# Unneeded products in four stage ends, and another order of copies, picks and routing in the latent attention

## The reference, cut to what matters

```python
x = _layernorm(x + L0_attn(x))                 # test-time training
x = _layernorm(x + L0_xattn(x, ctx, ctx))      # cross-attention, 32 query heads, 8 kv heads
x = _layernorm(x + L0_ffn(x))                  # silu(x@gate)*(x@up)@down, 1024 inner
x = _layernorm(x + L1_attn(x))                 # attention along the batch axis, 16 positions, causal
x = _layernorm(x + L1_xattn(x, ctx))           # latent cross-attention, 16 heads
x = _layernorm(x + L1_ffn(x))                  # 64 experts, 6 a token, 48 slots an expert, and a shared one
# L1_xattn: scores = (x Wq w_kc_q W_qr) . (rope(ctx) W_kr); softmax; times rope(ctx); w_kc_kv; Wo
# routing of L1_ffn: sigmoid(x@gate_w); best 4 of 8 groups; best 6 experts;
#   each expert keeps the first 48 of its tokens in token order
```

## Time and profile before

| | |
|---|---|
| time before, median of 3 runs | 1368.23 us (1364.22 to 1368.31) |
| the profiled execution | 1355.45 us, span 1353.6 us |
| mean granted TensorE clock | 0.963 |
| PE busy | 1198.9 us (89%) |
| DVE busy | 960.0 us (71%) |
| ACT busy | 550.5 us (41%) |

### The profile page before, as it was taken

How to read it: one execution, slowest core, us unless ns; L and a number is a source line. 1 busy time by engine, 2 the same in 40 slices (tenths; PEclk the granted TensorE clock), 3 DMA queues, 4 the chain that set the end, 5 groups by cost and what they waited for, 6 DMA issues and landing times. The chain is left out here.

```text
span 1353.6 us, 24642 instructions
## 1 busy us (share of the span) xinstructions
PE 1198.9 (89%) x9167; PEld 778.8 (58%) x9167; DVE 960.0 (71%) x2192; ACT 550.5 (41%) x1473; POOL 252.3 (19%) x327
## 2 busy tenths in 40 slices
PE   8799999999978989798998989886999999679964
PEld 3577788677743333245564457775777777334431
DVE  1699988699976777569984999863447688763325
ACT  3112112444426666564542210014777777232212
POOL 4000000122210111305431000110000000137761
PEclk9899999999989999999998989997999999899998
DMA  6211223200011332070001000006600000459557
GB/s 186 52 51 52 56 74 102 42 2 2 2 47 47 96 96 74 22 144 1 0 1 63 1 1 1 2 1 210 178 17 17 24 21 17 119 155 279 109 97 280
DMA packets 82851, 92.89 MB, mean 69 GB/s; under 512 B 25232, under 2 KB 66214, under 8 KB 82470
## 3 DMA queue, kind: packets, MB, share of 16 engines
q1 hardware_dynamic: 73820, 77.16, 19.4%
q0 software_dynamic: 6784, 10.43, 4.3%
q10 hardware_dynamic: 2128, 3.71, 0.8%
HBM read 68.91 MB, written 22.36 MB: 67 GB/s over the span
## 5 line engine op out<-in xcount | busy, mean ns | idle before, releaser
L400 DVE TENSOR_REDUCE gqa_x_slots<-gqa_scores 128x8 f32<-128x1024 f32 x64 | 78.4, 1226 | 35.3 <-PE gqa_scores L287 35.3
L1498 DVE TENSOR_REDUCE mla_neg_max<-mla_scores 128x8 f32<-128x1024 f32 x32 | 39.2, 1225 | 88.6 <-PE mla_scores L1369 62.8
L1447 ACT ACTIVATE mla_probs<-mla_scores,mla_neg_max 128x128 f32<-128x128 f32 x256 | 90.3, 387 | 6.1 <-DVE mla_neg_max L1498 6.1
L308 PE MATMUL gqa_scoresT<-gqa_x_slotsT,gqa_keys 32*128 32x512 f32 x256 | 72.9, 642 | 17.1 <-issue 15.1
L356 ACT ACTIVATE gqa_expT<-gqa_scoresT 128x1024 f32<-128x1024 f32 x64 | 65.6, 1024 | 38.7 <-PE gqa_scoresT L308 38.7
L2170 PE MATMUL ttt_z_ps<-ttt_prod,ident 128*128 128x256 f32 x288 | 70.9, 403 | 8.7 <-DVE ttt_prod L2246 8.7
L287 PE MATMUL gqa_scores<-gqa_keys_bd,xT 32*128 32x512 f32 x256 | 72.7, 665 | 4.2 <-DVE gqa_x_slots L400 2.3
L2170 PEld LDWEIGHTS ttt_z_ps<-ttt_prod,ident 128*128 128x128 f32 x288 | 55.3, 200 | 22.0 <-DVE ttt_prod L2246 14.7
L1359 PE MATMUL mla_q_ps<-xT,mla_to_keys 128*128 128x128 f32 x512 | 65.3, 283 | 1.5 <-PEq L63 1.5
L1359 PEld LDWEIGHTS mla_q_ps<-xT,mla_to_keys 128*128 128x128 f32 x512 | 62.3, 199 | 2.2 <-issue 2.1
L2177 PE MATMUL ttt_w_ps<-ttt_prod,ttt_neg_ident 128*128 128x144 f32 x448 | 58.9, 291 | 4.9 <-DVE ttt_prod L2279 4.9
(11 more groups left out here) (447 smaller groups left out, 2808.0 us busy)
## 6 DMA issues: line engine op xcount, KB each, us to landing
moe_w_gu<-in_moe_w_gu SPq DMA_DIRECT2D x24, 384.0 KB, 6.1
gqa_keys_bd<-in_gqa_keys_bd SPq DMA_DIRECT2D x16, 512.0 KB, 3.5
moe_w_dn<-in_moe_w_down SPq DMA_DIRECT2D x24, 192.0 KB, 7.0
moe_sums<-moe_zeros SPq DMA_DIRECT2D x2, 2176.0 KB, 11.4
xT<-in_x_feat SPq DMA_DIRECT2D x4, 512.0 KB, 7.4
ttt_k_by_head<-ttt_k_feat SPq DMA_DIRECT2D x8, 256.0 KB, 4.5
ttt_k_seq<-ttt_k_by_head SPq DMA_DIRECT2D x4, 512.0 KB, 3.8
x_tok<-in_mla_woT SPq DMA_DIRECT2D x8, 256.0 KB, 3.3
```

The lines of the kernel that those rows point to most:

```text
L308: ins = nc.tensor.matmul(scoresT[:, j % 2, :], keys[b % NBUF][group, c, :], x_slotsT[group, k % 2, :], start=True, stop=True)
L400: nc.vector.tensor_reduce(x_slots[:, b % 2, :, c * NJ + 2 * half:c * NJ + 2 * half + 2, HD].rearrange("p g j -> p j g"), scores[:, of].rea ...
L1447: ins = nc.scalar.activation(probs[:, k % NB, e, i, :], scores[:, k % 2, e, i, :], ACT.Exp, bias=neg_max[:, k % 2, e, i:i + 1], accum_out= ...
```

## The change

It does six things.

- Cross-attention: at step NU+3, between the last `turn_back` and the norm transposes of sequence 15, three f32 products.
- Feed-forward: eleven bf16 products ahead of the norm transposes of sequence 15.
- Batch axis: the transposes of 13 stand ahead of `out(15)` instead of behind it, with one f32 product between them; two f32 products stand between the transposes of 14 and 15.
- Latent attention, ACT: in steps 0 and 1 `copy_q(k+1)` stands ahead of `exponential(k)`.
- Latent attention, routing: the early picks are made in two parts, 256 keys in steps 20 and 21, and the other 256 with the first 48 results in steps 28 and 29, instead of 512 keys in steps 28 and 29; the first half's keys are turned at step 19 instead of 23; the parts of group 2 are spread otherwise over steps 30 to 34 (part 1 a step earlier, parts 2, 4 and 6 where they leave one later).
- Latent attention: at step 35, two f32 products.

```diff
@@ cross_attention_gqa, PE
                 if 0 <= k - 2 < NU:
                     weigh(k - 2)
+                if k == NU + 3:
+                    keep_busy(nc, scoresT[:, 0, :], keep["ident"][:], keys_bd[1][:, 0].rearrange("p g t -> p (g t)"), 3)
@@ gated_ffn_int8, PE
                 if sequence_at(n - 3) is not None:
+                    if sequence_at(n - 3) == B - 1:
+                        keep_busy(nc, gate_ps[:, 0], w_up[:, 0, 0, 0:P], x_parts[:, 0, 0, 0, :], 11)
                     norm.tensor(pe, sequence_at(n - 3))
@@ batch_axis_attention, PE
+            unused = w_qkv[:].rearrange("p c n -> p (c n)")[:, 0:512]
+            norm.tensor(pe, L - 3)
+            keep_busy(nc, wide_ps[:, 0, :], keep["ident"][:], unused, 1)
             out(L - 1)
-            for n in range(L - 3, L):
-                norm.tensor(pe, n)
+            norm.tensor(pe, L - 2)
+            keep_busy(nc, wide_ps[:, 0, :], keep["ident"][:], unused, 2)
+            norm.tensor(pe, L - 1)
@@ latent_cross_attention
-        ROUTE_LAG = 14
-        PARTS_AT = ((0,), (1, 2), (3, 4), (5, 6), (7,))
-        KEYS_AT, TOP_AT = (23, 27), (28, 29)
+        PARTS_AT = {14: (0, 0), 15: (0, 1, 2), 16: (0, 3, 4), 17: (0, 5, 6), 18: (0, 7),
+                    22: (1, 0), 23: (1, 1, 2), 24: (1, 3, 4), 25: (1, 5, 6), 26: (1, 7),
+                    30: (2, 0, 1), 31: (2, 2), 32: (2, 3), 33: (2, 4, 5), 34: (2, 6, 7)}
+        KEYS_AT = (19, 27)
+        TOP_AT = {20: (0, 0), 21: (0, 1), 28: (1, 0), 29: (1, 1)}
+        KEYS_LO, KEYS_HI = (0, moe.GK), (moe.GK, 2 * moe.GK + moe.CAP)
...
+                if k == LAST - 3:
+                    keep_busy(nc, scores[:, 0, 0].rearrange("t i n -> t (i n)"), keep["ident"][:], to_out[:, 0:2, :].rearrange("p c d -> p (c d)"), 2)
@@ latent_cross_attention, ACT
+                if k < 2:
+                    copy_q(k + 1)
                 if in_range(k):
                     exponential(k)
-                if in_range(k + 1):
+                if k >= 2 and in_range(k + 1):
                     copy_q(k + 1)
@@ latent_cross_attention, DVE
                 if k in TOP_AT:
-                    dve.wait_ge(moe.keys_copied, len(KEYS_AT))
-                    n = TOP_AT.index(k)
-                    for r in range(n * ROUNDS // 2, (n + 1) * ROUNDS // 2):
-                        moe.top_keys(order, moe.keys[:, moe.EARLY:], moe.EARLY, r)
+                    g, half = TOP_AT[k]
+                    dve.wait_ge(moe.keys_copied, g + 1)
+                    for r in range(half * ROUNDS // 2, (half + 1) * ROUNDS // 2):
+                        moe.top_keys(order, moe.keys[:, KEYS_HI[g]:KEYS_HI[g] + moe.CAP], KEYS_LO[g], KEYS_HI[g], r)
```

More of the change, by code:

```diff
@@ L1141, in __init__ @@
         self.zeros = sb("zeros", [P, self.W])
-        self.EARLY, self.PICKS = self.N // 4, self.N // 4 + self.CAP
-        self.keys, self.keys_left = sb("keys_by_expert", [P, self.PICKS]), sb("keys_left", [P, 2, self.PICKS])
+        self.GK, self.PICKS = self.N // 8, self.N // 4 + self.CAP
+        self.keys, self.keys_left = sb("keys_by_expert", [P, self.CAP + self.PICKS]), sb("keys_left", [P, 2, self.PICKS])
         self.keys_copied = sem("keys_copied")
@@ L1186, in load_experts, with top_keys @@
         sp.dma_start(down, self.io["moe_w_down"][q]).then_inc(self.w_loaded[n], 16)
-    def top_keys(self, order, out, width, r):
-        nc, eight = self.nc, out[:, 8 * r:8 * r + 8]
-        src = self.keys[:, 0:width] if r == 0 else self.keys_left[:, (r - 1) % 2, 0:width]
+    def top_keys(self, order, out, lo, hi, r):
+        nc, eight, width = self.nc, out[:, 8 * r:8 * r + 8], hi - lo
+        src = self.keys[:, lo:hi] if r == 0 else self.keys_left[:, (r - 1) % 2, 0:width]
         order(nc.vector.max(eight, src))
@@ L1323, in latent_cross_attention @@
         TURN_LAG, WEIGH_LAG = 2, 3
-        ROUTE_LAG = 14
-        PARTS_AT = ((0,), (1, 2), (3, 4), (5, 6), (7,))
-        KEYS_AT, TOP_AT = (23, 27), (28, 29)
+        PARTS_AT = {14: (0, 0), 15: (0, 1, 2), 16: (0, 3, 4), 17: (0, 5, 6), 18: (0, 7),
[4 more added lines that the diff above has]
+        KEYS_LO, KEYS_HI = (0, moe.GK), (moe.GK, 2 * moe.GK + moe.CAP)
+        KEYS_TO = (0, moe.GK + moe.CAP)
         ROUNDS = moe.CAP // 8
@@ L1467, in copy_keys @@
                 act.wait_ge(logits_ready, routed_at(KEYS_AT[g]) + 1)
-                nc.scalar.copy(moe.keys[:, g * 2 * T:(g + 1) * 2 * T], q_flat[:, 0:2 * T]).then_inc(moe.keys_copied, 1)
+                nc.scalar.copy(moe.keys[:, KEYS_TO[g]:KEYS_TO[g] + moe.GK], q_flat[:, 0:moe.GK]).then_inc(moe.keys_copied, 1)
             copy_q(0)
@@ L1515, in _ @@
                     norm.vector_end(dve, added_at(k))
-                g, at = (k - ROUTE_LAG) // moe.PARTS, (k - ROUTE_LAG) % moe.PARTS
-                if 0 <= g < moe.GROUPS - 1 and at < len(PARTS_AT):
-                    if g == at == 0:
+                if k in PARTS_AT:
+                    g, parts = PARTS_AT[k][0], PARTS_AT[k][1:]
+                    if g == 0 and 0 in parts:
                         dve.wait_ge(moe.loaded, moe.LOADED)
-                    for part in PARTS_AT[at]:
+                    for part in parts:
                         moe.route(dve, order, g, part)
                 if k in TOP_AT:
-                    dve.wait_ge(moe.keys_copied, len(KEYS_AT))
-                    n = TOP_AT.index(k)
-                    for r in range(n * ROUNDS // 2, (n + 1) * ROUNDS // 2):
-                        moe.top_keys(order, moe.keys[:, moe.EARLY:], moe.EARLY, r)
+                    g, half = TOP_AT[k]
+                    dve.wait_ge(moe.keys_copied, g + 1)
+                    for r in range(half * ROUNDS // 2, (half + 1) * ROUNDS // 2):
+                        moe.top_keys(order, moe.keys[:, KEYS_HI[g]:KEYS_HI[g] + moe.CAP], KEYS_LO[g], KEYS_HI[g], r)
 def mixture_of_experts(nc, keep, io, out, moe, latent):
@@ L1616, in _ @@
                         act.wait_ge(keyT_ready, B // 4)
-                        nc.scalar.copy(moe.keys[:, 0:moe.EARLY], keysT[:]).then_inc(moe.keys_copied, 1)
+                        nc.scalar.copy(moe.keys[:, moe.CAP:moe.CAP + 2 * moe.GK], keysT[:]).then_inc(moe.keys_copied, 1)
                     act.wait_ge(gate_ps_ready, g + 1)
@@ L1635, in _ @@
                 for r in range(ROUNDS):
-                    moe.top_keys(order, top, moe.PICKS, r)
+                    moe.top_keys(order, top, moe.CAP, moe.CAP + moe.PICKS, r)
                 order(nc.vector.tensor_copy(merged[:, 0, :], top[0:E, :]))
```

## The result

The changed kernel takes 1351.37 us (median of 7 runs, 1345.65 to 1355.24); the kernel before, run beside it, 1365.51 us (7 runs, 1361.71 to 1368.31). The ratio is 0.9914, with a 95% interval of 0.9889 to 0.9939, that is 8 to 15 us less, 11.7 in the middle (the two medians differ by 14.1). A second measurement beside three other kernels gave 0.9921 (0.9892 to 0.9951). The forecast was 1358.2, the direction faster, the range 1352 to 1365; the median lies 0.6 us under it. The forecast counted from 1368.23 for the kernel before, which took 1365.51 beside the changed one; set against 1368.23 the ratio gives 1356.5, inside the range.

What follows compares the result with a forecast made beforehand. TensorE was taken to bound the latent stage's full part, with low clock and idle around stage boundaries; 0.8 + 2.2 + 1.6 + 4.9 + 0 + 0.5 = 10.0 us less gave a median of 1358.2 us, range 1352 to 1365.

Steps and rivals of the forecast that it cites:

- Cross-attention filler: End of cross-attention: three products keep the clock up for feed-forward's start; 0.8 us, between 0 and 1.95.
- Feed-forward filler: End of feed-forward: eleven products keep the clock up for the batch-axis stage's start; 2.2 us, between 0 and 2.95.
- Batch drain: End of batch axis: earlier transposes of 13 and full clock end the stage 1.6 us sooner; lower end 0.
- Latent filling: Start of latent stage: query copies first bring score(3) sooner; 4.9 us, between 3.6 and 7.1.
- The walk at the full clock: Latent filling step by step from the first projection: score(3) at 17.3 us, 24.4 before.
- The 20.9 for the old order: Latent filling: score(3) at 20.9 us after the first projection in the old order at full clock.
- the 2.2 charged for one low stretch and a low start: Latent filling: 1.7 us for one low-clock stretch after long idle, 0.5 for a chance the stage starts low.
- Picks and parts: Latent routing: split picks cost about 1 us of DVE under saturated TensorE; gain 0, bounds 0 and 1.2.
- Latent filler: End of latent stage: two products speed the last transposes and router products; mixture starts 0.5 us sooner.
- The rival that the clock falls all the same: Barrier gaps and short idles still lower the clock; only the orders pay, 5.0 us, 1363.2; chance 0.16.
- The rival that the filling gives nothing lasting: Latent stage starts at half clock, so the order's 3.6 is nearly gone; sum 5.1, 1363.1; chance 0.13.
- Late fillers: All drains: fillers at low clock end late, 8.8 us against 5.0 from the orders, 1372.0; chance 0.05.

Runs made afterwards that it cites:

- the first pair: One profiled execution each of the kernel before and the changed kernel: 1355.45 us and 1352.29 us.
- fillers alone: Kernel before plus all the unneeded products, real work in the old order; ratio to the kernel before 0.9978 (0.9943 to 1.0012).
- one copy: Changed kernel with copy_q(2) back behind exponential(1); one execution, first projection to score(3) 19.78 us, to score(31) 219.85.
- third copy: Changed kernel with copy_q(3) and both copy_turned of unit 0 also ahead of exponential(2); one execution, score(3) 14.66 us after first projection, score(31) 215.77.
- orders alone: Changed kernel without any of its unneeded products; ratio to the kernel before 0.9963 (0.9930 to 0.9996).
- 22 products: Changed kernel with 22 instead of 11 unneeded products ending feed-forward; one execution, last stretch to the batch stage 6.89 us instead of 5.02.

## Why the prediction was right

Right in direction, and in the mechanism of the larger terms; the sum was 10.0 us, the stages of the first pair give 12.4 and the ratio 11.7. Three terms were too small, one was too large, and the split of the largest was wrong, so part of the agreement is luck. The lower end of the sum, 5.2, takes 1.6 for the batch drain, though the step itself puts its lower end at 0. By its steps:

- **Cross-attention filler, 0.8 "even".** It ends ahead of the transposes, as said. The clock of feed-forward's first 3.5 us was 1.00 in six of ten traces with the filler and about 0.55 in four, and 0.50 to 0.56 in all four without. Up to feed-forward's sequence 14 this is hard to see, since the four traces without a filler differ by 2.7 us among themselves (142.6 to 145.4). Up to its first transposes, those of sequence 0, it is plain; the kernel before and the changed one have them at

```profile
615.05 0.38 PE L183 MATMUL ff_normT<-ident,ff_n_normed 128*128 128x128 f32 x2
```

```profile
616.74 0.38 PE L183 MATMUL ff_normT<-ident,ff_n_normed 128*128 128x128 f32 x2
```

that is 40.64 and 38.69 us after the stage's first product (574.41 and 578.05). The six traces have 38.7 to 38.9 there, the four 40.4, and those without a filler 40.4 to 41.7. Against the mean of these last, 41.1, the filler is worth about 2.3 when it works and 1.7 on average over all ten; in the first pair it worked, and the 0.8 was low by 1.1. The 0.2 of the faster transposes did not come on top: the barrier behind them took 1.75 instead of 1.54.

- **Feed-forward filler, 2.2.** Too low: 2.94, the upper bound, in every trace. The error was to let the 1.48 us of the barrier take a share; at this place it lowered nothing.
- **Batch drain, 1.6.** 1.33 and 0.25: right. The rule by which a low clock costs half its length (the Trainium skill, "TensorE: Matmul & The Clock Gate", Terms) would have given an estimate of 2.55 for the earlier trace rows's 5.1 us. This case does not agree: what came back is 1.6, the order's share included, and 0.6 and 0.25 with the fillers alone, where TensorE is busy 2.75 us of the 5.1.
- **Latent filling, 4.9.** 5.7 to score(3) in the first pair, 6.0 by score(31). The walk at the full clock was right to 0.4 us where the clock stayed up (17.0 against 17.3, score(2) with one copy 12.7 against 12.8, the third copy 14.7 against 14.3). The split was not: "3.6 come from the order and 3.5 from the clock" took the clock for the fillers' gift, while the order alone gave 5.5 and 4.6 in the two traces, since behind waits of 0.68 us instead of 2.76 and 2.10 it did not fall again. The 20.9 for the old order is also 0.4 too much: the prediction's own prices give 2.9 to the first score and 5.85 a unit, 20.45 at score(3), so 3.1 and 4.0. And the 2.2 charged for one low stretch and a low start came by another way in the first pair, where the long wait cost nothing and the low start cost 1.7 (18.66 against 17.00). Where the long wait did cost, it was 1.54, behind score(3).
- **Picks and parts, 0.** Right, though "about 1 us of DVE" was too little: between score(3) and score(31) the picks alone take about 2.7 us more, and DVE is busy 4.0 us more in the windows of the full part. The cover held, TensorE was busy 203.00 of 203 us. In the parts of group 2, part 1 goes a step earlier, parts 4 and 6 a step later, and part 2 stays.
- **Latent filler, 0.5.** Wrong, 0. The step took it that TensorE's last products set the barrier, but SyncE's stores were last. The router products did start 0.3 us sooner after score(31) than before, and they did so without the filler too.

The rival that the clock falls all the same is refuted at the batch stage's start, in ten traces of ten; it came true at feed-forward's start in four of ten and at the latent stage's in two. The rival that the filling gives nothing lasting has its condition met in orders alone, where the first projection took 3.75 us: score(3) still came 5.5 us sooner and score(31) 5.8. Late fillers cost as told, shown with 22 products; the change's own were in time.

What stays open is why the latent stage sometimes begins low. With the batch fillers eight of ten traces begin at 1.00, and two (the changed kernel's first, 2.88 us for the projection, and fillers alone, 3.44) below 0.7; the first of these has the same waits as the eight. Nor was each filler of the batch drain run by itself.

## What to carry to other kernels

When a pipeline fills, put the copy that feeds the next product ahead of the long activation whose result is wanted only two steps later, then walk the next steps until the wait comes back elsewhere: two copies won 3.5 to 6 us by score(31), a third 1.5 to 2.9, and there a new wait of 0.83 showed. Unneeded products in a drain pay where work behind the barrier is bound by TensorE and waits for nothing else; let them end before the last input is ready, and rather take a few too few: five did as well as eleven here, in one trace, while what is too much is paid in full. Before speeding up a stage's last products, look at every engine's last instruction ahead of the barrier, the queue of stores too.

## What the runs showed of the hardware

- The same idle row leads to both levels. The wait of 2.55 us ahead of score(3) was followed by a low clock in three of six executions of the same code, and barrier gaps of 1.48 and 1.75 us in some and not in others. Even 3.65 us ahead of the latent stage's last transposes left them at 0.41 us in one kernel and at 0.66 in another. The waits of 0.68 us in the filling were never followed by a fall; the seven of 1.89 to 2.92 us ahead of score(1) and score(2), in the old order and with one copy, were each followed by one.
- MAX8 took 0.43 us over 256 keys, 0.48 over 304 and 0.69 over 512; MATCH_REPLACE8 0.41, 0.46 and 0.68, with 0.09 for the load of the values each time. Two halves cost about a third more than one whole.
- One execution says little of the whole kernel: identical code of the batch stage's middle took 178.8 to 182.2 us, the expert loop 147.1 to 152.2.
